# Router weights split in the first attention's early steps, two weight buffers with exchanged roles in the second attention

## The chip, the core and the metric

The kernel runs on one core of a Trainium2 chip. The metric is the time of one execution on the device in microseconds (us). TensorE (PE in the profile) multiplies matrices, VectorE (DVE), ScalarE (ACT) and GpSimd (POOL) work on rows of 128 partitions, and SyncE (SP) issues the DMAs. Each engine runs its own instructions strictly in the order in which they are written; between engines only semaphores order the work.

## What is computed

Four layers, each an attention over a shared context and a feed-forward part, each added to the stream `x` (16 batches of 64 rows, 512 features) through a gate. The change touches the first two layers:

```python
x = x + tanh(g_xattn[0]) * L0_xattn(layernorm(x), ctx, ctx, Wq, Wk, Wv, Wo)   # 32 heads of 16, 8 key heads
x = x + tanh(g_ffn[0])   * L0_ffn(layernorm(x), Wb, bias, Wr, A, Bm)          # dense x @ Wb.T + bias, plus top-2 of 8 experts of rank 16
x = x + tanh(g_xattn[1]) * L1_xattn(layernorm(x), ctx, wq, wk, wv, wo, ln_w)  # rmsnorm(.)*ln_w, then attention
x = x + tanh(g_ffn[1])   * L1_ffn(layernorm(x), ...)                          # int8 gate/up/down
```

Products are taken in float32 precision by splitting each operand into a high part (rounded to fp32r) and a low part (the rest) and adding three products: high*high, low*high, high*low.

## The kernel before, in words

All weights go the same way: SP fetches a matrix into a raw buffer (`raw_q`, `raw_o` of 2048 columns, `raw_c` of 1024), ACT casts it to the high part in pieces of 512 columns (`split_high_scalar`, line 381, or a line of its own), POOL subtracts to get the low part (`split_low_gpsimd`, line 388, or its own line), and PE multiplies. The pairs of split buffers are `wq`, `wo` (4 pieces each) and `wc` (2 pieces). A raw buffer is fetched anew only when its low part is written.

`attention16` is the code of the first two attentions (`rms` false, then true). On every engine it has a start and a loop over n, of 32 steps and a few to drain. In step n, PE makes the scores of n (line 879), DVE the maximum and the sum (lines 787 to 801), ACT the exponential (663), POOL the scaled probabilities (599), and PE, three steps later, their transposes (887). POOL also spreads the keys (587) for the batch after next. In the first four steps the output weights are split (lines 696 and 606).

Into the late steps of the first attention the router of the feed-forward part is woven. DENSE_AT puts its tile 0 at step 25, tile 1 at 27, then 29, 31, 33, 34, 35. For a tile, DVE normalises (1749), PE transposes (1822), ACT and DVE split the result (1712, 1757), and one step later PE makes the router's logits (line 397, 128x256, out of `wc`). The first logits wait for both low parts of `wc`: `pe.wait_ge(k.lo_c, k.at("lo_c", 4))`. ACT casts the router's matrix in step 23 (`high_c`), POOL subtracts one piece in step 24 and one in step 25 (line 1681). Then `dense_tail` runs the dense product of eight tiles (1841) out of `wq`, and DVE adds to the stream (1797, 1799).

At the start of the second attention PE makes keys and values out of `wc`: keys of halves 0 and 1 and values of halves 0 and 1, twelve matmuls each, in banks 4 and 5 in turn. The values of a half need the copy of the keys out of the same bank (ACT, line 633). ACT then copies the values (639, two copies a half), scales the normalised tiles (647, made by DVE in line 751) and casts their transposes (308); DVE subtracts (317). PE transposes tiles (298), and after tile 3 waits for all of `lo_q` and for both value copies before it makes the first queries:

```python
        for t in range(T):
            ln_transpose_tensor(k, pe, t, k.xs_ready if rms else k.xn_ready)
            if t in (3, 5):
                if t == 3:
                    pe.wait_ge(k.lo_q, k.at("lo_q", 4))
                    pe.wait_ge(k.kv_sbuf, k.at("kv_sbuf", 6))
                queries(0, t // 2 - 1)
```

POOL's start there is: the low parts of `wc`, three powers for the norm of tiles 0 to 5 (line 247), one for tiles 6 and 7, two powers for the second norm (578), then the four low parts of `wq`.

## Time and profile before

| | |
|---|---|
| median of 3 runs | 1658.66 us (1656.87, 1658.66, 1658.82) |
| the profiled execution | 1655.67 us, of it the span of the trace 1653.8 us |
| PE busy | 1534.1 us, 93% of the span |
| DVE, ACT, POOL busy | 901.5, 699.4, 636.6 us |
| mean granted clock of TensorE | 0.982 of full speed |
| first attention's loop on POOL | from 46.9 us to 160 us |
| second attention's keys and values on PE | from 208.7 us to 220.2 us |

The table says where an engine is full, not what a wait costs: PE is close to full over the whole program, so an idle time of PE with nothing else to do is a loss of the same size, if the work behind it follows.

### The profile page before, as it was taken

To read this page: it belongs to the slowest core of one execution; us is meant where nothing else is said; L and a number is where in the kernel's file an instruction comes from. 1 tells how busy PE (TensorE), PEld (TensorE's weight loads), DVE (VectorE), ACT (ScalarE), POOL (GpSimd) and SP (SyncE) were. 2 spreads that over 40 slices of the span, in tenths; PEclk is the share of its full clock that TensorE was granted. 3 is DMA by queue.
4 is the path that set the end of the run, shared out by engine and by line. 5 is a ranking of instruction groups with operands and counts; after the bars stand their busy time and mean duration, and the time that the engine had idled before them with its cause. 6 is when DMAs were issued, how large, how long until landed. Compare 5 with 4: busy or idle time off the path is not lost.

```text
span 1653.8 us, 25537 instructions
## 1 busy us (share of the span) xinstructions
PE 1534.1 (93%) x8786; PEld 1217.7 (74%) x8786; DVE 901.5 (55%) x1805; ACT 699.4 (42%) x2005; POOL 636.6 (38%) x606
## 2 busy tenths in 40 slices
PE   5897989888699999999999999889899999999998
PEld 4565766567578888888888887667677777777776
DVE  5786668858621222222231124688766776776666
ACT  4443154435335444453544444543344333443442
POOL 3544145557423221331323132334644544444430
PEclk9998999999989999999999999999999999999998
DMA  5001001021211010100101011114312212112101
GB/s 211 26 1 51 20 26 39 1 99 45 53 50 52 14 52 1 65 26 28 36 17 52 1 52 50 40 44 111 107 52 64 77 52 71 59 58 71 30 14 52
DMA packets 27885, 81.41 MB, mean 49 GB/s; under 512 B 3248, under 2 KB 11952, under 8 KB 22768
## 3 DMA queue, kind: packets, MB, share of 16 engines
q1 hardware_dynamic: 26896, 79.44, 14.5%
q8 instruction: 78, 1.28, 0.3%
q14 instruction: 47, 0.39, 0.1%
q10 hardware_dynamic: 864, 0.30, 0.1%
HBM read 69.25 MB, written 10.49 MB: 48 GB/s over the span
## 4 chain that ended last, share of the span: by engine, by line
PE 52%; issue 12%; DVE 5%; POOL 3%; ACT 1%; POOLq 0%; DVEq 0%; ACTq 0%
PE bank L397 32%; PE bank L1342 7%; PE bank L1330 2%; PE pair L2404 2%; PE bank L2382 2%; PE pair L1311 2%; POOL wo_low L388 1%; PE bank L1319 1%; PE pair L397 1%; POOL wq_low L1067 1%; PE bank L2390 1%; POOL probs L1076 1%; DVE small L222 0%; DVE probs L2236 0%; DVE out_low L2266 0%
## 5 line engine op out<-in xcount | busy, mean ns | idle before, releaser
L397 PE MATMUL bank<-hid_high,wq_high 128*128 128x512 f32 (+1 forms) x640 | 255.0, 398 | 2.4 <-issue 2.2
L1252 DVE SCALAR_TENSOR_TENSOR x_stream<-bank,gates,x_stream 128x512 f32<-128x512 f32 x64 | 48.0, 751 | 351.6 <-PE bank L1342 351.6
L397 PE MATMUL bank<-hid_high,wq_low 128*128 128x512 f32 (+1 forms) x640 | 238.0, 372 | 0.0
L397 PE MATMUL bank<-hid_low,wq_high 128*128 128x512 f32 (+1 forms) x640 | 236.4, 369 | 0.0
L1076 POOL TENSOR_TENSOR probs<-probs,small 128x512 f32<-128x512 f32 x64 | 67.2, 1050 | 356.7 <-DVE small L1240 356.7
L2131 ACT ACTIVATE probs<-probs,small 128x64 f32<-128x64 f32 x256 | 86.1, 338 | 135.2 <-DVE small L2255 135.2
L397 PEld LDWEIGHTS bank<-hid_high,wq_high 128*128 128x128 f32 x640 | 120.9, 189 | 25.9 <-issue 5.0
L397 PEld LDWEIGHTS bank<-hid_high,wq_low 128*128 128x128 f32 x640 | 120.8, 189 | 22.7
L397 PEld LDWEIGHTS bank<-hid_low,wq_high 128*128 128x128 f32 x640 | 121.3, 190 | 20.5 <-issue 3.4
L1150 ACT ACTIVATE probs<-pair,small 128x128 f32<-128x128 f32 x256 | 90.7, 367 | 82.6 <-DVE small L1234 80.2
L599 POOL TENSOR_TENSOR probs<-probs,small 128x512 f32<-128x512 f32 x64 | 67.2, 1051 | 122.5 <-DVE small L801 122.3
L1342 PE MATMUL bank<-wo_high,out_high 128*128 128x512 f32 x256 | 105.2, 411 | 5.1 <-DVE out_low L1245 2.6
L1342 PE MATMUL bank<-wo_high,out_low 128*128 128x512 f32 x256 | 101.0, 394 | 0.0
L1342 PE MATMUL bank<-wo_low,out_high 128*128 128x512 f32 x256 | 100.6, 393 | 0.0
L2144 ACT CAST out_high<-pair 128x512 fp32r<-128x512 f32 x64 | 37.5, 586 | 133.8 <-PE pair L2404 133.8
L1163 ACT CAST out_high<-bank 128x512 fp32r<-128x512 f32 x64 | 37.6, 587 | 121.3 <-PE bank L1330 121.3
L879 PE MATMUL pair<-keys_t,queries_t 128*128 128x512 f32 x128 | 70.0, 631 | 17.4 <-POOL keys_t L587 12.2
L397 PE MATMUL bank<-wo_high,out_high 128*128 128x512 f32 x192 | 79.9, 416 | 3.5 <-DVE out_low L805 2.9
L397 PE MATMUL bank<-hid_high,wc_high 128*128 128x512 f32 x160 | 67.7, 423 | 15.8 <-POOL wc_low L388 14.2
L2234 DVE TENSOR_TENSOR probs_t<-bank,rope 128x512 f32<-128x512 f32 x64 | 43.8, 684 | 67.8 <-PE bank L397 67.8
L2273 DVE SCALAR_TENSOR_TENSOR x_stream<-bank,gates,x_stream 128x512 f32<-128x512 f32 x64 | 48.0, 750 | 54.3 <-PE bank L397 54.3
L397 PE MATMUL bank<-wo_high,out_low 128*128 128x512 f32 x192 | 75.9, 395 | 0.0
(351 smaller groups left out, 3985.5 us busy)
## 6 DMA issues: line engine op xcount, KB each, us to landing
raw_q<-in_L_wq SPq DMA_DIRECT2D x18, 1024.0 KB, 5.0
raw_o<-in_L_wo SPq DMA_DIRECT2D x18, 1024.0 KB, 4.9
values<-ctx_values SPq DMA_DIRECT2D x32, 256.0 KB, 3.9
values_t<-ctx_keys SPq DMA_DIRECT2D x8, 512.0 KB, 3.3
raw_c<-in_L_wkv SPq DMA_DIRECT2D x6, 512.0 KB, 3.4
raw_o<-in_L_wkv SPq DMA_DIRECT2D x5, 512.0 KB, 4.8
x_stream<-in_x SPq DMA_DIRECT2D x8, 256.0 KB, 9.7
ctx_keys<-raw_o SPq DMA_DIRECT2D x8, 256.0 KB, 2.0
```

The costliest lines, as they stand in the source:

```text
L397: last = k.nc.tensor.matmul(out, stationary(a, c), moving(b, c), start=n == 0, stop=n == total - 1)
L599: nc.gpsimd.tensor_tensor(E[:, n % RING], E[:, n % RING], z.broadcast_to([P, J, S]), ALU.mult).then_inc(k.p_ready, 1)
L879: nc.tensor.matmul(k.bank[n % 2][:], Q[:, p % 2, rp, b % 4, :, :], KBD[:, b % 2], start=True, stop=True).then_inc(k.s_psum, 1)
L1076: nc.gpsimd.tensor_tensor(E[:, n % RING], E[:, n % RING], z.broadcast_to([P, 4, P]), ALU.mult).then_inc(k.p_ready, 1)
L1150: last_exp = nc.scalar.activation(E[:, n % RING, i, :], k.bank[n % 2][:, i * P:(i + 1) * P], ACT.Exp, bias=sc[:, 128 + 4 * (n % 2) + i:129 ...
L1163: nc.scalar.copy(O2[0][:, n % 2], OP).then_inc(k.o_hi, 1)
L1252: nc.vector.scalar_tensor_tensor(xt, k.bank[7][:], gate, xt, ALU.mult, ALU.add).then_inc(k.x_done, 1)
L1342: last = nc.tensor.matmul(k.bank[7][:], O[s][:, n % 2, h, :], k.wo[m][:, h * D:(h + 1) * D], start=h == i == 0, stop=h == 3 and i == 2)
L2131: last_exp = nc.scalar.activation(E[:, n % RING, i, :], E[:, n % RING, i, :], ACT.Exp, bias=sc[:, 128 + 4 * (n % 2) + i:129 + 4 * (n % 2) ...
L2144: nc.scalar.copy(O2[0][:, n % 2], OP[:, n % 2]).then_inc(k.o_hi, 1)
L2234: nc.vector.tensor_tensor(first, src, wide(cos, 0, P), ALU.mult)
L2273: nc.vector.scalar_tensor_tensor(xt, k.bank[7][:], gate, xt, ALU.mult, ALU.add).then_inc(k.x_done, 1)
```

## The change

Three things. (1) In the first attention ACT casts the router's matrix in step 8, not 23, and POOL subtracts its two pieces in steps 10 and 11, not 24 and 25. (2) In the second attention `wq` and `wo` change roles: the query weights (and later the gate/up weights of the feed-forward part) are split into `wo`, the output weights (and the down weights) into `wq`. With that, ACT casts the query weights before it copies the keys, after a wait for the last projection of the first attention, and POOL subtracts them ahead of its powers for the norm. (3) The value copies move on ACT from ahead of the first scale of a tile to behind the second (half 0) and the third (half 1). No instruction is added or removed.

```diff
+    WQ, WO = (k.wo, k.wq) if rms else (k.wq, k.wo)
@@ gpsimd
         for p in range(k.early):
             ln_rstd_gpsimd(k, pool, p, p + 1 - k.early)
+        if rms:
+            split_low_gpsimd(k, pool, k.raw_q, WQ, 2048, k.hi_q, k.at("hi_q", 0), k.lo_q)
         for p in range(LATE if rms else 0):
             ln_rstd_gpsimd(k, pool, p, p - 2)
         last_rstd_gpsimd(k, pool)
...
-        split_low_gpsimd(k, pool, k.raw_q, k.wq, 2048, k.hi_q, k.at("hi_q", 0), k.lo_q)
+        else:
+            split_low_gpsimd(k, pool, k.raw_q, WQ, 2048, k.hi_q, k.at("hi_q", 0), k.lo_q)
...
-                if n in (24, 25):
-                    dense_low_c(n - 24)
+                if n in (10, 11):
+                    dense_low_c(n - 10)
@@ scalar
         split_high_scalar(k, act, k.raw_c, k.wc, 1024, k.hi_c)
-        for h in range(2):
-            act.wait_ge(k.kv_psum, k.at("kv_psum", h + 1))
-            nc.scalar.copy(k.kt[:, 512 * h:512 * h + 512], k.bank[4 + h][:]).then_inc(k.kv_sbuf, 1)
-        act.wait_ge(k.loaded_q, k.at("loaded_q", 16))
-        split_high_scalar(k, act, k.raw_q, k.wq, 2048, k.hi_q)
-        for h in range(2):
+
+        def high_q():
+            act.wait_ge(k.loaded_q, k.at("loaded_q", 16))
+            split_high_scalar(k, act, k.raw_q, WQ, 2048, k.hi_q)
+
+        def value_copies(h):
             act.wait_ge(k.kv_psum, k.at("kv_psum", h + 3))
             for e in range(2):
                 nc.scalar.copy(VTD[:, 8 * h:8 * h + 8, e, :],
                                k.bank[4 + h][:].rearrange("p (b n) -> p b n", b=8)).then_inc(k.kv_sbuf, 1)
+
+        if rms:
+            act.wait_ge(k.y_psum, k.at("y_psum", 0))
+            high_q()
+        for h in range(2):
+            act.wait_ge(k.kv_psum, k.at("kv_psum", h + 1))
+            nc.scalar.copy(k.kt[:, 512 * h:512 * h + 512], k.bank[4 + h][:]).then_inc(k.kv_sbuf, 1)
+        if not rms:
+            high_q()
+            for h in range(2):
+                value_copies(h)
         if rms:
             m = stats(k)
             for t in range(T + 2):
...
                     nc.scalar.activation(xn_tile(k, t), xn_tile(k, t), ACT.Copy,
                                          scale=m["rms"][:, t:t + 1]).then_inc(k.xs_ready, 1)
+                if t in (1, 2):
+                    value_copies(t - 1)
                 if t >= 2:
                     ln_high_scalar(k, act, t - 2)
...
-                if n == 23:
+                if n == 8:
                     high_c()
```

The rest of the diff renames buffers: `k.wq` becomes `WQ` and `k.wo` becomes `WO` in the products and splits of `attention16`, and in `quant_mlp` the two names change places.

How the order of instructions moves. First attention, POOL, steps 24 to 26 before (line 599 is the scaling of a step's probabilities, 587 the keys, 1691 a power for the router's norm, `wc_low` the router's low part):

```order
L599 TENSOR_TENSOR probs<-probs,small 128x512
L1681 TENSOR_TENSOR wc_low<-raw_c,wc_high 128x512
L599 TENSOR_TENSOR probs<-probs,small 128x512
L587 TENSOR_TENSOR keys_t<-keys_t,kmask 128x512
L1681 TENSOR_TENSOR wc_low<-raw_c,wc_high 128x512
L599 TENSOR_TENSOR probs<-probs,small 128x512
L1691 TENSOR_TENSOR small<-small 128x1
L1686 TENSOR_TENSOR wq_low<-raw_q,wq_high 128x512
```

and the same engine at steps 10 to 12 now (the lines are 603, 591, 1708 and 1698 there):

```order
L603 TENSOR_TENSOR probs<-probs,small 128x512
L1708 TENSOR_TENSOR small<-small 128x1
L1698 TENSOR_TENSOR wc_low<-raw_c,wc_high 128x512
L603 TENSOR_TENSOR probs<-probs,small 128x512
L591 TENSOR_TENSOR keys_t<-keys_t,kmask 128x512
L1698 TENSOR_TENSOR wc_low<-raw_c,wc_high 128x512
L603 TENSOR_TENSOR probs<-probs,small 128x512 x2
```

The two subtractions have left steps 24 and 25 and stand fourteen steps earlier. Second attention, ACT, its start before:

```order
L381 CAST wc_high<-raw_c 128x512 x2
L633 COPY keys_t<-bank 128x512 x2
L381 CAST wq_high<-raw_q 128x512 x4
L639 COPY values_t<-bank 128x8x64 x4
L647 ACTIVATE probs<-probs,small 128x512 x3
L308 CAST hid_high<-bank 128x4x128
```

and now:

```order
L381 CAST wc_high<-raw_c 128x512 x2
L381 CAST wo_high<-raw_q 128x512 x4
L651 COPY keys_t<-bank 128x512 x2
L662 ACTIVATE probs<-probs,small 128x512 x2
L643 COPY values_t<-bank 128x8x64 x2
L662 ACTIVATE probs<-probs,small 128x512
L643 COPY values_t<-bank 128x8x64 x2
L308 CAST hid_high<-bank 128x4x128
```

Two scales stand ahead of all value copies, and a third ahead of those of half 1. Second attention, POOL, its start before:

```order
L388 TENSOR_TENSOR wc_low<-raw_c,wc_high 128x512 x2
L247 TENSOR_TENSOR small<-small 128x2 x4
L578 TENSOR_TENSOR small<-small 128x6
L578 TENSOR_TENSOR small<-small 128x2
L388 TENSOR_TENSOR wq_low<-raw_q,wq_high 128x512 x4
```

and now:

```order
L388 TENSOR_TENSOR wc_low<-raw_c,wc_high 128x512 x2
L388 TENSOR_TENSOR wo_low<-raw_q,wo_high 128x512 x4
L247 TENSOR_TENSOR small<-small 128x2 x4
L581 TENSOR_TENSOR small<-small 128x6
L581 TENSOR_TENSOR small<-small 128x2
```

The four subtractions of the query weights stand ahead of the six powers. On PE, DVE and SP the order of instructions is the same as before, with buffers renamed.

## Rows read from the trace of the kernel before

**Rows 1.** Span and mean granted TensorE clock of the core
```profile
core 0: 1653.8 us, clock 0.982
```

**Rows 2.** PE in time, steps 26 to 29: start, us, engine, work, [idle before <-releaser]
```profile
125.86 0.60 PE L887 MATMUL bank<-ident,probs 128*128 128x128 f32 x4
133.98 0.55 PE L397 MATMUL bank<-wc_high,hid_high 128*128 128x256 f32 x1 [7.51 <-POOL wc_low L1681]
...
136.88 1.92 PE L879 MATMUL pair<-keys_t,queries_t 128*128 128x512 f32 x2
...
144.80 0.28 PE L397 MATMUL bank<-wc_high,hid_high 128*128 128x256 f32 x1
...
146.35 1.02 PE L879 MATMUL pair<-keys_t,queries_t 128*128 128x512 f32 x2
```

**Rows 3.** The stretch 134:137: length, busy of PE, PEld, DVE, ACT, POOL, clock, DMA
```profile
134.00:137.00 3.00, 3.00 (x14) 3.00 (x15) 0.00 (x0) 0.09 (x1) 0.00 (x0) 0.50 0.48 175
```

**Rows 4.** POOL in time, steps 10 to 12 and step 25
```profile
78.87 0.56 POOL L1691 TENSOR_TENSOR small<-small 128x1 f32<-128x1 f32 x1
80.85 1.04 POOL L599 TENSOR_TENSOR probs<-probs,small 128x512 f32<-128x512 f32 x1 [1.42 <-DVE small L801]
...
85.02 1.04 POOL L599 TENSOR_TENSOR probs<-probs,small 128x512 f32<-128x512 f32 x1 [2.12 <-DVE small L801]
...
132.57 1.26 POOL L1681 TENSOR_TENSOR wc_low<-raw_c,wc_high 128x512 fp32r<-128x512 f32 x1
```

**Rows 5.** DVE in time, steps 26 and 27
```profile
127.47 0.68 DVE L1757 TENSOR_TENSOR hid_low<-bank,hid_high 128x512 fp32r<-128x512 f32 x1
...
130.22 0.50 DVE L1749 TENSOR_SCALAR ctx_staging<-x_stream,small 128x512 f32<-128x512 f32 x1
...
138.83 0.69 DVE L787 TENSOR_REDUCE small<-pair 128x8 f32<-128x512 f32 x1 [1.42 <-PE pair L879]
```

**Rows 6.** ACT in time, step 8 and what follows it
```profile
66.42 0.63 ACT L663 ACTIVATE probs<-probs 128x512 f32<-128x512 f32 x1 [1.07 <-DVE probs L790]
69.64 0.59 ACT L670 COPY probs_t<-bank 128x512 f32<-128x512 f32 x1 [2.59 <-PE bank L887]
```

**Rows 7.** ACT in time, start of the second attention
```profile
195.32 1.14 ACT L381 CAST wc_high<-raw_c 128x512 fp32r<-128x512 f32 x2
212.11 0.59 ACT L633 COPY keys_t<-bank 128x512 f32<-128x512 f32 x1 [15.65 <-PE bank L397]
...
220.27 1.07 ACT L639 COPY values_t<-bank 128x512 f32<-128x512 f32 x2 [1.64 <-PE bank L397]
221.23 1.95 ACT L647 ACTIVATE probs<-probs,small 128x512 f32<-128x512 f32 x3
223.08 0.58 ACT L308 CAST hid_high<-bank 128x512 fp32r<-128x512 f32 x1
```

**Rows 8.** PE in time, its first transposes of the second attention
```profile
222.02 1.26 PE L298 MATMUL bank<-ident,probs 128*128 128x128 f32 x8 [1.78 <-ACT probs L647]
```

**Rows 9.** DVE in time, from the tail of the first feed-forward part
```profile
196.22 1.12 DVE L235 TENSOR_SCALAR small<-small 128x2 f32<-128x2 f32 x1
197.25 0.68 DVE L1797 TENSOR_TENSOR x_stream<-x_stream,probs 128x512 f32<-128x512 f32 x1
...
205.78 0.75 DVE L1799 SCALAR_TENSOR_TENSOR x_stream<-bank,gates,x_stream 128x512 f32<-128x512 f32 x1 [1.10 <-PE bank L1853]
...
216.41 1.41 DVE L751 SCALAR_TENSOR_TENSOR probs<-x_stream,small,values 128x512 f32<-128x512 f32 x2
```

**Rows 10.** POOL in time, the same stretch
```profile
196.02 3.06 POOL L388 TENSOR_TENSOR wc_low<-raw_c,wc_high 128x512 fp32r<-128x512 f32 x2 [16.56 <-ACT wc_high L381]
...
207.63 1.07 POOL L247 TENSOR_TENSOR small<-small 128x2 f32<-128x2 f32 x1 [4.57 <-DVE small L235]
...
217.68 4.99 POOL L388 TENSOR_TENSOR wq_low<-raw_q,wq_high 128x512 fp32r<-128x512 f32 x4
```

**Rows 11.** SP's issue of the second attention's query weights
```profile
156.56 0.33 SPq L376 DMA_DIRECT2D raw_q<-in_L_wq  x1
```

More of the change, by code:

```diff
@@ L682, in _ @@
         if not rms:
-            high_c, high_q, high, logits, exponent, gated = dense_scalar(k, act)
+            high_c, dense_high_q, high, logits, exponent, gated = dense_scalar(k, act)
         for n in range(N + LAG + 1 if rms else N + LAG + 2):
@@ L695, in _ @@
                 cols = slice(512 * n, 512 * n + 512)
-                nc.scalar.copy(k.wo[0][:, cols], k.raw_o[:, cols]).then_inc(k.hi_o, 1)
+                nc.scalar.copy(WO[0][:, cols], k.raw_o[:, cols]).then_inc(k.hi_o, 1)
             if n % 4 == 2 and n // 8 + 1 < 4:
@@ L701, in _ @@
             if not rms:
-                if n == 23:
+                if n == 8:
                     high_c()
                 if 24 <= n < 28:
-                    high_q(n - 24)
+                    dense_high_q(n - 24)
                 if n in DENSE_AT:
@@ L906, in project @@
             last = product(k, k.bank[7][:], lambda s, r: O[s][:, r, P * (t % 2):P * (t % 2) + P],
-                           lambda m, r: k.wo[m][:, r * D:(r + 1) * D], R)
+                           lambda m, r: WO[m][:, r * D:(r + 1) * D], R)
             last.then_inc(k.y_psum, 1)
@@ L2613, in _ @@
             if s == 2:
-                split_low_gpsimd(k, pool, k.raw_o, k.wo, 1024, k.hi_o, k.at("hi_o", 0), k.lo_o)
+                split_low_gpsimd(k, pool, k.raw_o, k.wq, 1024, k.hi_o, k.at("hi_o", 0), k.lo_o)
             if s in (3, 4):
@@ L2671, in _ @@
                 act.wait_ge(k.loaded_o, k.at("loaded_o", 16))
-                split_high_scalar(k, act, k.raw_o, k.wo, 1024, k.hi_o)
+                split_high_scalar(k, act, k.raw_o, k.wq, 1024, k.hi_o)
             if s == 3:
@@ L2871, in down @@
                     last = nc.tensor.matmul(k.bank[6][:], QTI[t % 2][:, c * P:(c + 1) * P],
-                                            k.wo[w][:, c * D:(c + 1) * D], start=c == w == 0, stop=c == w == 1)
+                                            k.wq[w][:, c * D:(c + 1) * D], start=c == w == 0, stop=c == w == 1)
             last.then_inc(k.y_psum, 1)
```

10 lines of the change are left out of this document (5 added, 5 removed).

## The prediction

> **What bounds the kernel now.** Read the core's row first: span 1653.8 us at a mean clock of 0.982 [rows 1]. The profiled execution took 1655.67 us, so 1.9 us lie around the span. It is 3.0 us under the median of the three runs, 1658.66, and their spread is 2 us; I form the sum on the trace and subtract it from the median. PE is busy for 93% of the span, so what can be won is its idle time, where the work behind it follows. I then read PE in time at the two places that the change touches, and asked at each which engine released it.
>
> Place A is step 26 of the first attention. PE finishes the transposes at 125.86 + 0.60 = 126.46 and starts the router's first logits at 133.98, after 7.51 us idle, released by POOL's low part of the router's matrix [rows 2]. That subtraction began at 132.57 and ended at 133.83 [rows 4]. The 0.15 us between its end and PE's start say that it is indeed what PE waited for. The clock then stands at 0.50, which is 1.2 GHz [rows 3], with PE idle before it; the scores that follow take 1.92 us against 1.02 us at 2.4 GHz [rows 2].
>
> Place B is the start of the second attention. PE ends its keys and values at about 220.2 us: ACT's copies of the last values start at 220.27, released by PE. ACT then makes two copies (1.07 us), and only behind them scales the first tiles, at 221.23 [rows 7]. PE's transposes start at 222.02 after 1.78 us idle, released by that scale [rows 8]. ACT's first cast of a transpose comes behind three scales in a row, at 223.08 [rows 7].
>
> **Part 1, the router's matrix split early.** What it removes: the wait for POOL. What is late next is the other operand of the first logits, the low part of tile 0, which DVE starts at 127.47 and ends at 128.15 [rows 5]. With the 0.15 us of the hand-over PE starts at 128.3 instead of 133.98: 5.7 us. Next comes the speed behind the wait. PE now stands for 1.8 us (126.46 to 128.3) instead of 7.5. At place B it also stood 1.78 us [rows 8], and the 1.26 us that eight transposes take there are not the length of a slow clock; so I expect the full clock here. At 2.4 GHz the twelve logits and the values' transpose take 146.35 - 144.80 = 1.55 us [rows 2]. So the scores of step 27 start at about 128.3 + 0.1 + 1.55 = 129.95 and end at 129.95 + 1.02 = 130.97. DVE is free by then: its normalising of tile 1 ends at 130.22 + 0.50 = 130.72 [rows 5]. The maximum of step 27 starts at 131.0 instead of 138.83 [rows 5]: 7.8 us. From there DVE and ACT carry the chain as before, at the same distances, and POOL has less to do. Bounds: 5.7 us, if PE stays slow after all, and 8.2 us, if the transposes behind the scores, slow before, also shorten the chain. I take 7.8, since two separate instructions are followed to it.
>
> What it adds: two casts on ACT in step 8 and two subtractions on POOL in steps 10 and 11. ACT's exponential of step 8 ends at 67.05 and it then stands for 2.59 us, until 69.64 [rows 6]. The two casts take 1.14 us, as the same pair does in [rows 7], so they are hidden with 1.4 us to spare. On POOL the power of step 10 ends at 78.87 + 0.56 = 79.43; the subtraction of 1.26 us ends at 80.7, and the next probabilities come at 80.85 [rows 4]. That is a cover of 0.15 us. In step 11 POOL has the probabilities and the keys (about 1.04 us each, to 82.9), so the subtraction ends at 84.2, ahead of 85.02 [rows 4]. If a subtraction takes 1.5 us, as half of the pair of 3.06 us in [rows 10], step 10 is late by 0.1 us. Bounds 0 and 0.3; I take 0. SP's fetch of the next `raw_c` moves forward with the low part; nothing queued behind it on SP becomes free by that, and nothing used it in the meantime.
>
> **Part 2, the query weights split ahead.** ACT has cast `wc` by 195.32 + 1.14 = 196.46 and then waits for PE until 212.11, 15.65 us [rows 7]. Four more casts of about 0.55 us fit into it. The two waits ahead of them are for the last projection of the first attention, done before the dense tail, and for a transfer issued at 156.56 [rows 11], 40 us earlier. What is queued behind them are the copies of the keys, for which PE waits; they keep their times. On POOL the four subtractions (4.99 us where they stand now [rows 10]) follow `wc_low` from 199.1 to about 204.1, or to 205.2 if each takes 1.53 us as in the pair of 3.06 us [rows 10]. The first two powers then end by 207.3, and the third had to wait for DVE until 207.63 anyway [rows 10]. So the norm is not late. `lo_q` was no wait of PE: it ended at 217.68 + 4.99 = 222.67 [rows 10], and PE's first queries come after four transposes. Alone, part 2 brings about nothing. But with part 3 the queries would want it about 2 us earlier, and POOL would be close; here it is the cover for part 3.
>
> **Part 3, the value copies between the scales.** DVE has tiles 0 and 1 normalised before it starts tile 2 at 216.41 [rows 9]. ACT scales both (1.95 / 3 = 0.65 us each [rows 7]), copies the values of half 0 when PE has them (the third of four equal products between 208.7 and 220.2, so about 217.4) until 218.5, and scales tile 2 until 219.2. All of it ends before PE does. PE's transposes of tiles 0 and 1 follow the values without the 1.78 us [rows 8]. ACT copies half 1 from 220.27 to 221.3 and casts the first transpose then, not at 223.08 [rows 7]: 1.8 us. DVE, PE and ACT then hand each other the tiles at the same distances. POOL's subtractions, which ran from 217.68 on beside DVE, are gone there, which may give 0.2 us more. Bounds 0 and 2.2; I take 1.85.
>
> **The shared port.** In the tail POOL's pair of subtractions takes 3.06 us while DVE adds to the stream (line 1797, two operands in SBUF), and a DVE instruction on two columns takes 1.12 us beside it [rows 9, 10]. Four subtractions take 4.99 us where DVE runs little [rows 10], 2.5 us a pair. The Trainium skill (SBUF — State Buffer, Who interferes with whom) says that DVE with two inputs in SBUF, or in a two-port mode, and a GpSimd instruction that reads SBUF exclude each other for a whole instruction. By that rule, the trace agrees: both engines are the longer for the overlap. It speaks against part 2, which puts four subtractions into this stretch; the price is the second rival's below.
>
> **Sum.** 7.8 + 0 + 0 + 1.85 = 9.65 us. On the profiled execution that is 1655.67 - 9.65 = 1646.0; on the median 1658.66 - 9.65 = 1649.0 us, the forecast.
>
> **The rivals.** (1) *The clock stays low behind the shorter wait.* PE stands 1.8 us there and had been light in work before. For it: the clock was at 0.50 only after such a pause [rows 3]; against it: 1.78 us at place B. Then part 1 gives 5.7: 1658.66 - 5.7 - 1.85 = 1651.1 us.
>
> (2) *DVE is held up by POOL in the tail.* At worst each subtraction holds it for its whole length, 4.99 us, of which the 1.10 us that it stands idle before 205.78 [rows 9] take one part: 3.9 us late. Tile 1 is ready by 216.4, so ACT's first two scales end at about 216.8; the half 0 copies can start at 217.4, and the third scale ends 1 us before PE does; so 0.6 + 1.0 = 1.6, say 1.7 us of lateness cost nothing and 2.2 us remain. Part 3 then gives 1.85 - 2.2 = -0.35, together 7.45: 1651.2 us. What speaks against the worst: beside the pair of [rows 10] the small DVE instruction took 1.12 us in all, and POOL bore the rest.
>
> (3) *The wait at step 26 goes to another.* If a further condition of the logits came at 133.9 as well, only part 3 would count: 1656.8 us. The low part of tile 0 is there at 128.15 [rows 5], and the code names no third.
>
> (4) *Slower: the clock falls more often in all that follows.* Everything behind step 26 shifts by 8 to 10 us, and where PE pauses the clock may fall at other places. A mean of 0.982 [rows 1] means 0.018 x 1653.8 / 0.5 = 60 us at 1.2 GHz. Each further 2 us there cost PE 1 us of work, so it takes 20 us more to eat the gain and 26 us more to be 0.2% slower, 1661.9 us or above. Against it: a shift helps as often as it harms.
>
> **How the numbers follow.** The forecast has 0.72, rival 1 has 0.10, rival 2 in its full size 0.08, part 3 without any gain (1650.9) 0.03, rival 3 0.04, rival 4 0.03. 0.2% are 3.3 us, about what a measurement of this kernel can tell from no change. Faster are all but the last two, 0.93; rival 3 is within, 0.04; slower is 0.03. The range goes from 1645 (8.2 and 2.2 us, and the 3 us by which single executions lie lower) to 1653 (5.7 us and nothing else).
>
> **What would show it.** In the trace after: PE's logits of tile 0 start about 128.3, released by DVE, with a pause under 2 us before them and the clock at 1.0 behind; the maximum of step 27 at 131.0; the probabilities of steps 11 and 12 on POOL still at 80.9 and 85.0; in the second attention, with all times about 7.8 us earlier, ACT's query casts near 189, the keys' copies behind a wait for PE, PE's transposes without a pause after the values, and ACT's first cast of a transpose 9.6 us earlier than 223.08. Wrong would be: a pause of PE at the logits with another releaser; a clock of 0.5 behind it; POOL's probabilities late at step 11; or DVE starting tile 0 of the second norm later than 7.8 us before its old time by over 1.7 us.

## The result, and the profile after

The changed kernel takes 1650.63 us, the median of five runs (1648.45 to 1652.17). The kernel before takes 1657.71 us over the five runs that stand beside it (1656.87 to 1658.82). The ratio is 0.9954 with a 95% interval of 0.994 to 0.9969: faster by 7.6 us, at least 5.1 and at most 9.9. Predicted were 1649.0 us and a gain of 9.65. The time lies inside the range of 1645 to 1653; the forecast is 1.6 us too low. The profiled execution took 1649.76 us against 1655.67 of the one before, 5.9 us less. That is under the 7.1 us between the two medians, because the profiled execution of before was 2 us faster than its own median. The core stands as follows:

```profile
core 0: 1647.9 us, clock 0.981
```

All times of this profile behind 61 us carry an offset of their own: in this execution the clock fell to 1.2 GHz between 56 and 61 us, ahead of anything that the change touches, where it had not before. DVE's first subtraction behind it, first before and then after:

```profile
61.40 0.29 DVE L778 TENSOR_TENSOR values<-bank,vmask 128x128 f32<-128x128 f32 x1 [1.17 <-PE bank L871]
```

```profile
62.52 0.29 DVE L795 TENSOR_TENSOR values<-bank,vmask 128x128 f32<-128x128 f32 x1 [2.23 <-PE bank L888]
```

DVE's steps are 1.12 us later from there on. I take that off where I compare instants with before.

**Place A**, PE in time, against [rows 2]:

```profile
126.98 0.60 PE L904 MATMUL bank<-ident,probs 128*128 128x128 f32 x4
129.32 0.39 PE L397 MATMUL bank<-wc_high,hid_high 128*128 128x256 f32 x1 [1.74 <-DVE hid_low L1774]
...
130.97 1.02 PE L896 MATMUL pair<-keys_t,queries_t 128*128 128x512 f32 x2
```

The pause before the first logits is 1.74 us instead of 7.51, and DVE's low part of tile 0 ends it. The scores behind take 1.02 us for the pair, not 1.92. The table of stretches (start and end, length, then for PE, PEld, DVE, ACT and POOL the busy time and the number of instructions, then clock, DMA share and GB/s) has the clock at 1.00 there, and at 1.00 from 117 to 134 us too, against 0.50 in [rows 3]:

```profile
134.00:137.00 3.00, 3.00 (x14) 2.16 (x14) 2.22 (x6) 1.96 (x5) 2.65 (x3) 1.00 0.00 0
```

DVE's maximum of step 27, against [rows 5]:

```profile
132.03 0.69 DVE L804 TENSOR_REDUCE small<-pair 128x8 f32<-128x512 f32 x1
```

That is 132.03 against 138.83, or 6.80 us earlier; without the offset of 1.12 us it would be earlier still, so place A gives 6.80 + 1.12 = 7.92 us. Forecast were 7.8. POOL in steps 10 and 11, where the low parts now stand, against [rows 4]:

```profile
80.54 1.29 POOL L1698 TENSOR_TENSOR wc_low<-raw_c,wc_high 128x512 fp32r<-128x512 f32 x1
81.99 1.04 POOL L603 TENSOR_TENSOR probs<-probs,small 128x512 f32<-128x512 f32 x1 [0.15 <-DVE small L818]
...
83.99 1.28 POOL L1698 TENSOR_TENSOR wc_low<-raw_c,wc_high 128x512 fp32r<-128x512 f32 x1
```

The probabilities come at 81.99, which is 80.87 in the time of before (80.85 there), and still wait for DVE for 0.15 us, the cover that the prediction had counted.

**The tail before place B.** POOL and DVE in time, against [rows 9, 10]; first POOL, then DVE:

```profile
189.22 3.07 POOL L388 TENSOR_TENSOR wc_low<-raw_c,wc_high 128x512 fp32r<-128x512 f32 x2 [16.57 <-ACT wc_high L381]
192.24 6.00 POOL L388 TENSOR_TENSOR wo_low<-raw_q,wo_high 128x512 fp32r<-128x512 f32 x4
```

```profile
192.66 1.42 DVE L1814 TENSOR_TENSOR x_stream<-x_stream,probs 128x512 f32<-128x512 f32 x1
194.12 0.75 DVE L1816 SCALAR_TENSOR_TENSOR x_stream<-pair,gates,x_stream 128x512 f32<-128x512 f32 x1
...
195.72 0.78 DVE L235 TENSOR_SCALAR small<-small 128x2 f32<-128x2 f32 x1
```

The four subtractions take 1.50 us each beside DVE, not the 1.25 of [rows 10], and one of DVE's adds takes 1.42 us instead of 0.68, one of its small instructions 0.78 instead of 0.17. DVE falls 1.39 us behind: the add that stood at 201.83 comes at 196.42, only 5.41 us earlier, after 6.80 at 132. By 202.6 DVE has made that good in two waits for PE that stood there anyway: that of 1.10 us is gone, one of 1.26 us has become 0.93, and its instants are 6.81 us earlier again.

**Place B**, ACT in time, against [rows 7]:

```profile
210.74 1.07 ACT L643 COPY values_t<-bank 128x512 f32<-128x512 f32 x2 [0.75 <-PE bank L397]
211.70 0.74 ACT L662 ACTIVATE probs<-probs,small 128x512 f32<-128x512 f32 x1
213.47 1.07 ACT L643 COPY values_t<-bank 128x512 f32<-128x512 f32 x2 [1.03 <-PE bank L397]
214.43 0.60 ACT L308 CAST hid_high<-bank 128x512 fp32r<-128x512 f32 x1
```

ACT's first cast is at 214.43 instead of 223.08. From the start of the last value copies to it there are 0.96 us now and 2.81 before, so the change gives 1.85 us here, as forecast. Up to this instant the two parts have brought 7.92 + 1.85 = 9.77 us; less the offset of 1.12 that is the 8.65 us between the two instants. What comes then is in PE's rows, against [rows 8]:

```profile
213.27 1.03 PE L298 MATMUL bank<-ident,probs 128*128 128x128 f32 x8
215.90 0.63 PE L298 MATMUL bank<-ident,probs 128*128 128x128 f32 x4 [1.60 <-DVE hid_low L317]
217.16 0.97 PE L298 MATMUL bank<-ident,probs 128*128 128x128 f32 x4 [0.63 <-ACT probs L662]
...
228.59 1.96 PE L896 MATMUL pair<-keys_t,queries_t 128*128 128x512 f32 x4 [1.80 <-ACT queries_t L675]
```

PE starts its transposes with no pause behind the values (1.78 us before). But it pauses for 1.60 and 0.63 us between the tiles, and then four transposes take 0.97 instead of 0.63 us: the clock has fallen to 1.2 GHz, and the stretch shows it (0.66 on average):

```profile
216.00:221.00 5.00, 4.37 (x24) 4.16 (x25) 4.29 (x7) 3.24 (x6) 0.00 (x0) 0.66 0.00 0
```

In the profile of before the first query products ran at full clock. Its fourth tile, whose four transposes take 0.63 us, and its first scores:

```profile
225.96 0.63 PE L298 MATMUL bank<-ident,probs 128*128 128x128 f32 x4 [0.81 <-ACT probs L647]
...
235.87 1.96 PE L879 MATMUL pair<-keys_t,queries_t 128*128 128x512 f32 x4 [1.80 <-ACT queries_t L658]
```

From the last value copies to the first scores it is 15.12 us after (228.59 - 213.47) and 15.60 before (235.87 - 220.27); so at the scores only 0.48 of the 1.85 us are left in this pair of profiles. Behind them the distance between the two executions wanders with the stretches at 1.2 GHz: after is ahead by 7.3 us at 223, by 5.2 at 345, 7.6 at 466, 8.9 at 1065, 5.5 at 1179 and 5.9 at the end.

### The profile page after: what moved, and what is told of

Read it like the earlier page. It is cut to its first block, busy times and chain, and to the rows that moved or that the text cites. A ratio compares the mean times of both kernels' runs of the same rounds, so it can differ in the third digit from the quotient of the medians.

```text
span 1647.9 us, 25538 instructions
## 1 busy us (share of the span) xinstructions
PE 1535.1 (93%) x8786; PEld 1219.6 (74%) x8786; DVE 902.5 (55%) x1805; ACT 699.4 (42%) x2005; POOL 637.4 (39%) x606
## 4 chain that ended last, share of the span: by engine, by line
PE 52%; issue 12%; DVE 5%; POOL 3%; ACT 1%; POOLq 0%; DVEq 0%; ACTq 0%
PE bank L397 32%; PE bank L1359 7%; PE bank L1347 2%; PE pair L2421 2%; PE pair L1328 2%; PE bank L2399 2%; POOL wo_low L388 1%; PE pair L397 1%; PE bank L1336 1%; POOL wq_low L1084 1%; PE bank L2407 1%; POOL probs L1093 1%; DVE probs L2253 0%; DVE out_low L2283 0%; DVE probs L2252 0%
## 5 line engine op out<-in xcount | busy, mean ns | idle before, releaser
L397 PE MATMUL bank<-hid_high,wq_high 128*128 128x512 f32 (+1 forms) x576 | 235.5, 409 | 2.4 <-issue 2.2
L397 PE MATMUL bank<-hid_high,wq_low 128*128 128x512 f32 (+1 forms) x576 | 220.7, 383 | 0.0
L397 PE MATMUL bank<-hid_low,wq_high 128*128 128x512 f32 (+1 forms) x576 | 219.1, 380 | 0.0
L397 PEld LDWEIGHTS bank<-hid_high,wq_high 128*128 128x128 f32 x576 | 109.6, 190 | 24.1 <-issue 3.2
L397 PEld LDWEIGHTS bank<-hid_high,wq_low 128*128 128x128 f32 x576 | 109.3, 190 | 22.7
L397 PEld LDWEIGHTS bank<-hid_low,wq_high 128*128 128x128 f32 x576 | 109.8, 191 | 19.8 <-issue 2.6
L1359 PE MATMUL bank<-wo_high,out_high 128*128 128x512 f32 x256 | 104.6, 408 | 5.1 <-DVE out_low L1262 2.6
L1359 PE MATMUL bank<-wo_high,out_low 128*128 128x512 f32 x256 | 100.3, 392 | 0.0
L687 ACT COPY probs_t<-bank 128x512 f32<-128x512 f32 x64 | 37.6, 588 | 85.4 <-PE bank L904 85.3
L1262 DVE TENSOR_TENSOR out_low<-bank,out_high 128x512 fp32r<-128x512 f32 x64 | 44.2, 691 | 52.2 <-ACT out_high L1180 52.2
```

The source lines that it names most:

```text
L397: last = k.nc.tensor.matmul(out, stationary(a, c), moving(b, c), start=n == 0, stop=n == total - 1)
L687: nc.scalar.copy(PT[:, b % 2, :, P * (n % 2):P * (n % 2) + P], k.bank[2 + n % 2][:].rearrange("p (i n) -> p i n", i=4)).then_inc(k.pt_sbuf, 1)
L1262: nc.vector.tensor_tensor(O2[1][:, n % 2], OP, O2[0][:, n % 2], ALU.subtract).then_inc(k.o_lo, 1)
L1359: last = nc.tensor.matmul(k.bank[7][:], O[s][:, n % 2, h, :], k.wo[m][:, h * D:(h + 1) * D], start=h == i == 0, stop=h == 3 and i == 2)
```

## The experiments

Each kernel stands against before on the same chip. Where I give distances, they run from one named instruction to another in one profile, so that what came earlier in that execution drops out.

**One part alone.** The router's weights split early, nothing else:

```diff
-                if n in (24, 25):
-                    dense_low_c(n - 24)
+                if n in (10, 11):
+                    dense_low_c(n - 10)
...
-                if n == 23:
+                if n == 8:
```

> Part 1 alone (router's matrix cast in step 8, subtracted in steps 10 and 11; the second attention as before). Theory: the wait of 7.5 us and the slow clock behind it go, so the maximum of step 27 starts 7.8 us earlier, measured against step 20 of the same trace, and the time falls by 7.8 us, 1.5 us either way for where the clock falls afterwards: ratio 0.9944 to 0.9962. Rival (the clock behind step 26 stays low): 5.7 us, 0.9966. Rival (another wait takes its place): 0.999 to 1.001.

Measured: 1652.51 us against 1657.77, ratio 0.9962 (0.9949 to 0.9976), or 6.3 us, between 4.0 and 8.5; that is the lower edge of what was expected, and close to the rival's 0.9966. The distance decides between them. From DVE's first subtraction of the step at 61 us to the maximum of step 27 it is 69.50 us; before has 77.43 and the full change 69.51. So 7.93 us come from this part at place A, and the clock behind the shorter wait is high; the total keeps less of them. At the start of the second attention nothing was changed in it, and yet the first query products are slow:

```profile
215.50 1.27 PE L298 MATMUL bank<-ident,probs 128*128 128x128 f32 x8 [1.78 <-ACT probs L647]
218.02 1.00 PE L298 MATMUL bank<-ident,probs 128*128 128x128 f32 x4 [1.25 <-DVE hid_low L317]
219.45 1.08 PE L298 MATMUL bank<-ident,probs 128*128 128x128 f32 x4 [0.44 <-ACT probs L647]
```

Last value copies to first scores: 16.56 us, against 15.60 in the profile of before with the same code and the same pauses of 1.78 and 1.25 us (the third is 0.44 for 0.81, since the transposes ahead of it already run slow). So the fall of the clock at this place doesn't need the new order of ACT. In this profile a second slow stretch follows at 245 us, where before had none.

**The other two parts, without the first.** The exchange of `wq` and `wo` with the early split, and the value copies between the scales:

```diff
+    WQ, WO = (k.wo, k.wq) if rms else (k.wq, k.wo)
...
+                if t in (1, 2):
+                    value_copies(t - 1)
```

> Parts 2 and 3 alone (the second attention changed, the router's matrix as before). Theory: ACT's first cast of a transpose comes 1.85 us earlier, measured against PE's last product of the values; PE's queries keep it only if TensorE's clock does not fall between: ratio 0.9982 to 1.0002. Rival (the gain there is real and the clock has no part): 0.9989 with a start of the scores 1.85 us earlier in the trace.

Measured: 1656.41 us (11 runs) against 1657.77, ratio 0.999 (0.9981 to 0.9999), between 0.2 and 3.1 us, 1.4 us by the medians. From the last value copies to the first cast it is 0.95 us (2.81 before); to the first scores 15.09. Against the profile with the old order in which the clock fell too, 16.56, this is 1.47 us. The total lies within what was expected. Added up, the two ratios give 8.0 us and the two differences of medians 6.6; the full change shows 7.6 and 7.1.

**The full change once more.**

> The changed kernel once more. Theory (the low stretches of TensorE's clock lie elsewhere in each execution): the parts of the trace up to ACT's first cast of a transpose stand at the same distances as in the first profile, within 0.1 us, but the stretches at 1.2 GHz lie at other places than 216 to 221, 316 to 341 and 446 to 457 us; ratio 0.994 to 0.997. Rival (the places are fixed by the program): a stretch at 1.2 GHz again at the first queries of the second attention.

Measured: 1649.83 us, ratio 0.9956 (0.9942 to 0.997). Distances 0.96 and 15.10 us, as in the first profile. The time at 1.2 GHz within the span is 69 us here against 62 (one expectation below has 62 to 76 us for the first six profiles; within the spans it is 60 to 74). Many of the stretches stand a few microseconds off, but the one at the first queries is back (216 to 219). The expectation had it wander like the others; it missed.

**Without the moved value copies.** Parts 1 and 2:

```diff
-                if t in (1, 2):
-                    value_copies(t - 1)
...
+        for h in range(2):
+            value_copies(h)
```

> Parts 1 and 2 without part 3: the value copies stand ahead of the scales again. Theory: part 2 alone brings nothing; PE waits 1.78 us for the first scale as before, and ACT's first cast of a transpose stands 2.8 us behind the start of the last value copies (before: 223.08 - 220.27), against 0.96 in the changed kernel. Rival (the early split itself gains): less than 2.0 us.

Measured: 1653.33 us in one run; last value copies to first cast 2.81 us, to first scores 16.52. Casting and subtracting the query weights early brings nothing at this place, and one total can't tell more; the clock fell at the first queries here as well, and again at 243 us.

**Without the exchange.** Parts 1 and 3, the query casts back behind the key copies:

```diff
-    WQ, WO = (k.wo, k.wq) if rms else (k.wq, k.wo)
+    WQ, WO = k.wq, k.wo
...
+        high_q()
```

> Parts 1 and 3 with the weight buffers left in their old roles: ScalarE's four query-weight casts stay behind the key copies of the second attention, and only the value copies move between the scales. My account says that the early split is only cover and brings next to nothing: worked out from the rows of before, the casts end at 217.49, two scales of 0.70 and the first two value copies bring ScalarE to 219.9, one scale to 220.5, the last two value copies to 221.5 us, so its first cast of the transposed stream starts about 1.6 us earlier than with the copies ahead of the scales (of 1.85 with the swap), and the low pieces, ready at 222.67 in before's time, come before the first query products want them. Expected: 1.6 us between TensorE's last value product and that cast against 1.4 with the swap and 3.0 in before; span within 1 us of the full change apart from the clock. The rival is that the swap is what makes room: then the cast comes less than 1 us earlier than in before (2.3 us or more), or TensorE waits for the low pieces before its first query product. The run can't tell differences under 2 us by its total; the distances decide.

Measured: 1649.54 us in one run, ACT in time:

```profile
208.29 2.18 ACT L381 CAST wq_high<-raw_q 128x512 fp32r<-128x512 f32 x4
210.38 1.33 ACT L656 ACTIVATE probs<-probs,small 128x512 f32<-128x512 f32 x2
211.62 1.06 ACT L640 COPY values_t<-bank 128x512 f32<-128x512 f32 x2
212.56 0.73 ACT L656 ACTIVATE probs<-probs,small 128x512 f32<-128x512 f32 x1
213.25 1.07 ACT L640 COPY values_t<-bank 128x512 f32<-128x512 f32 x2
214.21 0.60 ACT L308 CAST hid_high<-bank 128x512 fp32r<-128x512 f32 x1
```

PE begins the transposes, behind its last value product, at 213.06, and the cast comes 1.15 us later; with the exchange it is 214.43 - 213.27 = 1.16. I had expected 1.6 here; ACT is just in time without the exchange, with no pause left. From the last value copies to the cast it is 0.96 us, so the place shows the full 1.85 us. The low pieces hold up nobody: POOL ends them at 215.68, and PE's first query product stands at 217.68, behind the fourth tile. The prediction called part 2 the cover for part 3. That is not so: it isn't needed.

**The second low piece one step earlier only.** Before, with one edit:

```diff
-                if n in (24, 25):
-                    dense_low_c(n - 24)
+                if n == 24:
+                    dense_low_c(0)
+                    dense_low_c(1)
```

> Before, with one edit: GpSimd makes both low pieces of the router weights in step 24 of the first attention and none in step 25, so the second piece is ready one step earlier, but still late. If the lateness of that piece is what holds the first router products, TensorE starts them as soon as GpSimd ends it: from the rows of before about 127.07 + 2.55 = 129.6, so 129.7 us against 133.98, and VectorE's maximum of step 27 stands about 71 us behind VectorE's first subtraction of the step that reads 61.40 in before (77.43 there, 69.51 with the split at steps 10 and 11): most of the 7.9 us gained, with 1.5 to 2 left. If the gain came from taking the work out of GpSimd's late steps at all and not from the piece being ready, the distance stays near 77; if the clock in the pause is what counts, TensorE still shows 1.2 GHz from about 130 us and the distance is 74 or more.

Measured: 1655.65 us in one run. PE in time, and the stretch behind:

```profile
130.19 0.36 PE L397 MATMUL bank<-wc_high,hid_high 128*128 128x256 f32 x1 [3.24 <-POOL wc_low L1682]
...
132.66 1.76 PE L880 MATMUL pair<-keys_t,queries_t 128*128 128x512 f32 x2
```

```profile
130.00:134.00 4.00, 3.81 (x15) 3.07 (x16) 1.46 (x4) 1.47 (x4) 2.27 (x3) 0.59 0.39 131
```

POOL's pair ran from 127.56 to 130.04, and PE started 0.15 us behind it: it is this piece, and when it is there, that holds the logits. The distance to the maximum of step 27 is 72.55 us, a gain of 4.88 where I expected about 6.4. The missing 1.5 us are clock: behind a pause of 3.24 us it fell 0.5 us into the logits, which took 2.47 us with the values' transpose against 1.55 in [rows 2], and the scores 1.76 against 1.02.

**TensorE kept at work in the pauses of place B.** The full change, and transposes of the identity that nobody reads:

```diff
             ln_transpose_tensor(k, pe, t, k.xs_ready if rms else k.xn_ready)
+            if rms and t in (1, 2):
+                for _ in range(12 if t == 1 else 4):
+                    nc.tensor.transpose(k.bank[0][:, 0:P], k.ident[:], k.ident[:])
```

> The full change, with TensorE transposing the identity into a free bank in its two pauses at the start of the second attention: 12 times behind the second tile's transposes (12 x 0.12 = 1.5 us in a pause of 1.60) and 4 times behind the third's (0.5 in 0.63). These are extra work whose result nobody reads. If the pauses are what lets the clock fall to 1.2 GHz at the first query products (0.98 level over the execution, but 1.2 GHz at 216 to 221 in both profiles of the full change), the clock stays at 2.4 GHz there, and the first scores start 13.7 us behind ScalarE's last pair of value copies instead of 15.1: 1.4 us less in the span. If the low stretch comes at a time of its own, whatever TensorE does in the pauses, the distance stays at 15.1 or the stretch lies just elsewhere; if the extra transposes get in the way, the second or third tile's transposes start later than 2.43 us behind ScalarE's last pair of value copies. Total expected 1649.2 against 1650.6 of the full change, where low stretches elsewhere are the same; they may take it back.

Up to the first scores it did what was expected: they come 13.60 us behind the last value copies (225.20 and 211.60), 1.50 us sooner than in the full change, and the clock stays up.

```profile
225.20 1.95 PE L896 MATMUL pair<-keys_t,queries_t 128*128 128x512 f32 x4 [1.80 <-ACT queries_t L675]
```

But the stretch at 1.2 GHz has only moved, to 240 us. The two stretches in this kernel, and then in the full change:

```profile
214.00:228.00 14.00, 11.23 (x81) 9.56 (x82) 8.73 (x14) 7.32 (x14) 0.00 (x0) 1.00 0.00 1
234.00:248.00 14.00, 11.69 (x67) 7.96 (x68) 9.44 (x20) 5.77 (x11) 10.05 (x10) 0.88 0.35 113
```

```profile
214.00:228.00 14.00, 10.57 (x75) 9.91 (x73) 7.59 (x12) 8.52 (x17) 0.00 (x0) 0.88 0.01 1
234.00:248.00 14.00, 10.95 (x71) 7.85 (x70) 10.96 (x23) 6.15 (x12) 12.62 (x13) 1.00 0.18 53
```

A mean of 0.88 over 14 us is 3.4 us at 1.2 GHz in the one place or in the other, and by DVE's step at 246 us the 1.5 us are given back. Then the time is 1656.14 us over 12 runs (1653.21 to 1660.78), ratio 0.9989 (0.9979 to 0.9998), where 1649.2 was expected: 5.5 and 6.3 us above the two medians of the full change. That comes from later places. The profile is that of the slowest of the 12 executions, so it shows about twice what the median loses. Against the second profile of the full change it is 2.3 us behind at 457, 5.6 at 778, 7.0 at 1106 and 11.6 at 1398. The jump at 778 in PE's rows:

```profile
773.50 0.48 PE L1331 MATMUL pair<-keys_t,queries_t 128*128 128x128 f32 x2 [0.33 <-issue]
776.42 1.65 PE L1331 MATMUL pair<-keys_t,queries_t 128*128 128x128 f32 x6 [2.44 <-issue]
```

PE stands for 2.44 us in the middle of eight equal products, which no engine holds up, and the six behind it and the products that follow run at 1.2 GHz. From 773 to 777 us only the instruction queues moved anything, three packets. The likeliest reading is that PE waits there for its own instructions, and that 16 more of them at 211 us put a piece of the stream at a bad place 560 us later. It is not shown: the full change has as many packets on these queues from 755 to 800 us (eight in its second profile) and no such pause. The next two runs bear on it.

**TensorE kept at work in the tail too.** As above, and in three pauses of steps 27, 28 and 31 of the second attention:

```diff
+        def busy(count):
+            pe.wait_ge(k.q_sbuf, k.at("q_sbuf", 8))
+            for _ in range(count):
+                nc.tensor.transpose(k.bank[4][:, 0:P], k.ident[:], k.ident[:])
...
+            if rms and n == 28:
+                busy(9)
...
+            if rms and n in (27, 31):
+                busy(10 if n == 27 else 18)
```

> As the run before it, and TensorE also transposes the identity in three pauses at the end of the second attention: 10 times in the 1.42 us pause of step 27, 9 in the 1.27 us pause of step 28, 18 in the 2.44 us pause of step 31. Behind these pauses both profiles of the full change show 1.2 GHz, at 316 to 323 and 332 to 341 us, where twelve products of a projection take 0.43 us each instead of 0.23 (2.4 us per projection). If pauses bring the clock down, both stretches go, and the end of the second attention comes 4 to 5 us earlier relative to its start: 1644.5 in all. If the clock has a budget of its own (62 to 76 us at 1.2 GHz in each of the six profiles so far), the time at 1.2 GHz stays in that band and turns up elsewhere, and the total stays within 1.5 us of 1650.

Measured: 1645.48 us, ratio 0.9923 (0.991 to 0.9936), 13.0 us under the before of its comparison, and 4.35 and 5.15 us under the two medians of the full change. PE at step 27 and 28:

```profile
311.02 1.26 PE L944 MATMUL bank<-ident 128*128 128x128 f32 x10
312.61 0.64 PE L915 MATMUL bank<-probs_t,values 128*32 128x256 f32 x8 [0.33 <-issue]
313.18 1.20 PE L944 MATMUL bank<-ident 128*128 128x128 f32 x9
314.51 1.13 PE L896 MATMUL pair<-keys_t,queries_t 128*128 128x512 f32 x2
```

and the stretches:

```profile
312.00:324.00 12.00, 11.04 (x64) 6.72 (x63) 9.98 (x22) 5.86 (x12) 10.65 (x10) 1.00 0.00 1
326.00:336.00 10.00, 7.63 (x49) 5.23 (x48) 5.43 (x13) 3.26 (x7) 7.45 (x7) 1.00 0.16 55
```

The clock stays at 2.4 GHz through both. The time at 1.2 GHz is 58 us in this profile, and 60 and 62 in the other two with a filled tail; in the nine profiles of changed kernels without one it is between 62 and 84. The mean clocks of all executions, turned into time as in the prediction, say it better: 58 to 59 us in the three kernels with a filled tail, 67 in the full change. So the slow time did not all turn up elsewhere, unlike at place B, and the rival of a fixed budget falls.

**The same stream without the work.** The 37 transposes of the tail replaced by 74 waits that are already met:

```diff
-            for _ in range(count):
-                nc.tensor.transpose(k.bank[4][:, 0:P], k.ident[:], k.ident[:])
+            for _ in range(2 * count):
+                pe.wait_ge(k.q_sbuf, k.at("q_sbuf", 8))
```

> The kernel with the filled tail, with the 37 transposes of the identity at the end of the second attention replaced by 74 waits that are already met (one for each load and one for each multiplication), so that TensorE's instruction stream is as long and its pauses of 1.42, 1.27 and 2.44 us stay idle; the 16 transposes at the start of the attention stay. The run with those 16 alone lost 3.7 us in a pause of 2.44 us in the middle of L1331's products, put down to issue, with packets on the instruction queue around it, and some 4 us more near 1386 us in the same way; the run with the filled tail had neither. If it is the work in the pauses that keeps the clock up in the tail, the stretches at 1.2 GHz near 316 and 332 us are back, and the time is about 3 to 5 us above the filled tail's 1645.5: 1649 to 1650. If the filled tail gained only because the longer stream put the fetches elsewhere, the tail's stretches stay away or the time stays at 1645.5. The pauses for issue near 772 and 1386 us should be as small as in the filled tail (under 0.6 and 1.3 us) if they come from where the instruction stream is cut, and large again if they come from the 16 transposes.

Measured: 1648.95 us over four runs, ratio 0.9943 (0.9928 to 0.9958), 3.5 us above the filled tail (its four times, 1648.3 to 1650.01, lie above all five of the other, though the intervals of the ratios touch). PE's pauses and the slow stretches are back:

```profile
313.58 0.64 PE L915 MATMUL bank<-probs_t,values 128*32 128x256 f32 x8 [1.57 <-DVE values L795]
315.68 2.05 PE L896 MATMUL pair<-keys_t,queries_t 128*128 128x512 f32 x2 [1.46 <-POOL keys_t L591]
```

```profile
312.00:324.00 12.00, 8.96 (x44) 5.45 (x44) 8.35 (x18) 4.84 (x10) 8.78 (x9) 0.86 0.00 1
328.00:336.00 8.00, 5.05 (x22) 3.54 (x23) 4.75 (x11) 2.48 (x5) 6.56 (x6) 0.79 0.01 2
```

From 241 to 333 us it falls 3.9 us behind the filled tail. So the work in the pauses keeps the clock up. The slow time in these two stretches is 6.7 us here and 13.6 in the first profile of the full change, and the kernel is 0.9 to 1.7 us faster than that; this part of the filled tail's gain is not the work's, and its cause stays open. And there is no pause for issue near 772 or 1386 us, with the same 16 transposes at place B: what cost the kernel with these alone its 6 us went away with 77 more instructions in the stream. That fits the reading above; which piece of the stream is fetched when was not measured.

**The shortest edit with the filled pauses.** Parts 1 and 3 without the exchange, and the same 53 transposes:

> Parts 1 and 3 without the exchange of the weight buffers, with the same 53 transposes of the identity in TensorE's pauses: the shortest edit that should hold all of the gain. If the early split of the query weights is worth nothing, the time is that of the filled tail with the exchange, 1645.5 within 1 us, and ScalarE's first cast stands 1.15 us behind TensorE's last value product as without fillers. If the exchange has a value that the single run without it hid, it is slower by 1 us or more.

Measured: 1647.07 us, ratio 0.9933 (0.9919 to 0.9946), 1.6 us above the version with the exchange; ranges overlap (1645.88 to 1651.08 and 1643.91 to 1647.26). The expected 1 us was missed. The profile has a pause of 2.7 us for issue at L2405 near 1380 us, and the two executions part by 4.3 us there (from 1.4 at 1377 to 5.7 at 1386); up to 394 us they keep within 1.3. So nothing is seen of a value of the exchange at its place; five executions of each can't tell whether the 1.6 us are real.

**Only the tail filled.** The kernel with 53 transposes without the 16 at place B:

```diff
-            if rms and t in (1, 2):
-                for _ in range(12 if t == 1 else 4):
-                    nc.tensor.transpose(k.bank[0][:, 0:P], k.ident[:], k.ident[:])
```

> The full change with the 37 transposes of the identity in the three tail pauses of the second attention, and without the 16 at its start. In the four profiles with those 16 the stretch at 1.2 GHz was gone from the first queries (216 to 221 us) but stood at 238 to 242 us instead, and by 245 us nothing was left of the 1.5 us. If the start's filling only moves the stretch, this kernel is as fast as with both, 1645.5 within 1.5 us: the clock falls again near 216 us, not near 240, the first scores stand 15.1 us behind the last value copies, and near 315 and 332 us the clock stays at 2.4 GHz. If the start's filling was worth its 1.5 us, this kernel takes 1647 us or more. It also has a stream that is 32 instructions shorter; a pause for issue of over 2 us that neither of the two has would show that as the cause of a longer time.

Measured: 1646.30 us, ratio 0.9916 (0.9903 to 0.993), the best ratio of this study; the before of its comparison is 1659.04. The stretches:

```profile
214.00:228.00 14.00, 10.66 (x76) 10.00 (x74) 7.50 (x12) 8.54 (x17) 0.00 (x0) 0.88 0.00 1
234.00:248.00 14.00, 10.95 (x72) 7.94 (x71) 10.96 (x23) 6.07 (x12) 12.60 (x13) 1.00 0.18 52
312.00:324.00 12.00, 11.25 (x68) 7.50 (x69) 10.16 (x22) 6.06 (x12) 10.71 (x10) 1.00 0.01 2
```

The slow stretch is at the first queries again and gone from 240 us, the first scores stand 15.13 us behind the last value copies, and the tail is at 2.4 GHz. Filling place B brings nothing that can be told; filling the tail brings what the two together do.

## Why the prediction was right, and what was mis-sized

**What bounds the kernel.** Right. PE's two pauses had the releasers that the rows named, and taking them away moved all that follows.

**Part 1.** Right in size and in steps at its place: 7.92 us (7.93 alone) for 7.8. DVE's low part of tile 0 releases the logits (pause 1.74 us for 1.8), the clock stays up in all ten profiles with this part, the cover on POOL is 0.15 us, ACT's two casts are hidden. The half step of the sixth experiment shows the mechanism at another dose.

**Part 2.** Right as a number, 0; wrong as an account. The fifth experiment has the whole 1.85 us without it. My step "POOL would be close" looked at the low pieces alone; they are ready ahead of PE's first query product either way, and ACT fits the four casts between its key copies and the scales.

**Part 3.** Right where it acts: from the last value copies to the first cast it is 0.95 to 0.97 us in all nine profiles that have this part, and 2.81 in all four that do not. The prediction's steps came to 1.8 us and it took 1.85, so that it fits to the hundredth is luck. Behind the cast it said that "DVE, PE and ACT then hand each other the tiles at the same distances", and that holds only as far as the clock does. From the last value copies to the first scores:

| | clock high at the first queries | clock low there |
|---|---|---|
| old order | 15.60 (before) | 16.52, 16.56, and 17.82 with a longer slow stretch |
| new order | 13.60 to 13.64 (four profiles, pauses filled) | 15.09 to 15.19 (five profiles) |

High on both sides, the gain at the scores is 2.0 us; low on both sides it is 1.3 to 1.5, and more against the longer stretch; in the first pair of profiles, high before and low after, 0.48.

**The sum.** 9.65 us were forecast; 7.1 came by the medians and 7.6 by the ratio. The interval of 5.1 to 9.9 doesn't exclude the sum, so the total doesn't refute it. The time came out nearer to the forecast (1.6 us) than the gain did (2.6), by luck: the five runs of before have a median 0.95 us lower than the three from which the forecast was taken. The terms at the two places measured 7.92 and 1.85. What the sum left out is a term for the clock behind them: it assumed that all that follows keeps its speed. The single runs say that both parts lose on the way: part 1 has 7.93 us at place A and 6.3 in the total (5.3 by the medians), parts 2 and 3 have 1.85 at the cast and 1.6 or so in the total (1.4 by the medians). By these middle values the greater loss stands behind part 1; both intervals reach the full value, so it is not shown where the missing 2 us went.

An estimate of the clock's share: the mean clock of ten executions of the change gives 67 us at 1.2 GHz. Before has 71 us in the first comparison (13 executions, without two whose clock of 0.93 and 1.0 lies far off) and 75 in the second (17 executions). So the change has 4 to 8 us less, though place A alone was slow for 10 us (130 to 140 us in the profile of before). Elsewhere it has 2 to 6 us more, which is 1 to 3 us of PE's work, and that would cover what is missing. The profile from which the distances were taken could not show it: at a clock of 0.982 it had 60 us at 1.2 GHz, less than a usual execution, and it is the only one of nine profiles with idle pauses at place B in which the first queries ran at full clock.

**The rivals.** (1) Clock low behind the shorter wait: fell, 1.00 behind 1.74 us; behind 3.24 us it is so. (2) DVE held up by POOL: the mechanism is there, the price is not. DVE was late by 1.39 us at most where the rival had up to 4.99, its waits for PE took all of it, and place B shows the full 1.85 us. The rows are 1.50 us for 1.25 on POOL, and on DVE 1.42 us for 0.68 in one add while others beside the subtractions kept 0.68. The Trainium skill (SBUF — State Buffer, Who interferes with whom) has a DVE instruction with two inputs in SBUF and a GpSimd one that reads SBUF contend for a shared pair of ports. The rows of the slow add agree. (3) Another wait at step 26: fell. (4) The clock falls more often later: in its full size it fell, since the kernel is faster. In a small form it may be what is missing, by the estimate above; the two profiles of the change have 62 and 69 us at 1.2 GHz against 60 before, and no longer the 10 us of place A.

## What to carry to other kernels

Follow each gain to the first instruction of the next stage, and ask of the pauses left on the way what the clock does behind them; a distance from one profile holds only for the clock that it happened to have. Where TensorE pauses a microsecond or two for other engines, a few transposes into a free bank can keep the clock up: here 37 in three pauses gave 3.5 us over the same stream without the work, but 16 in two others only moved the slow stretch on. Extra instructions can also cost far from where they are added, so time the whole kernel and compare with one whose stream is as long.

## What was unexpected of the hardware

The same kernel shows the same total at 1.2 GHz only roughly (62 and 69 us), with stretches that differ from one execution to the next, and the two profiled executions of the change drift against each other by up to 4 us. The slow stretch at place B came in eight of nine profiles with idle pauses there (1.60 and 0.63 to 0.66 us, or 1.25 and 0.36 to 0.81). In all four with filled ones it was gone and one stood at 239 to 244 us instead; the two kernels with part 1 and the old order of the copies have both, one at the first queries and one at 243 to 249.

Sixteen more transposes at 211 us went with a pause of PE of 2.44 us at 774 and one of 2.29 us at 1389 us, each time with the clock low behind it; 77 instructions more left no such pause at either place, and the kernel without the exchange, with all 53 transposes, has one of 2.66 us near 1380 again.
